# Softmax loop of a fused token-embedding, attention and expert kernel: VectorE's order regrouped, the probabilities' bits moved to ScalarE, two-operand multiplies for the small scalars

## The reference, cut to what matters

```
x_int = x_int - x_int.max(axis=-1, keepdims=True)
x0_int = floor(-0.6931 / scale);  x_int = maximum(x_int, 30 * x0_int)
q = floor(x_int / x0_int);  r = x_int - x0_int * q
exp_int = floor((r * (r + b_int) + c_int) * exp2(30 - q))
sm = round(exp_int.sum(axis=-1, keepdims=True) / exp_int)
big = floor(log2(sm));  big = where(sm - exp2(big) >= exp2(big - 1), big + 1, big)
attn = where(big >= 16, 0, exp2(-clip(big, 0, 15)))
o = attn @ v
```

## Time and profile before

| | us |
|---|---|
| median of three runs | 1189.9 (1189.35 to 1193.78) |
| the profiled execution, its own time | 1189.11 |
| its span | 1187.3 |
| softmax loop, first distances to the end of its barrier | 434.0 to 703.8 |

### The profile page before, as it was taken

The page is one execution under the profiler, slowest core; times in us unless marked ns, Lnnn a source line. Parts: engine busy times, 40 slices in busy tenths (PEclk is TensorE's granted clock), DMA queues, the critical chain, the costliest instruction groups (busy, mean ns, idle before and its releaser), DMA issues.

```text
span 1187.3 us, 25829 instructions
## 1 busy us (share of the span) xinstructions
PE 803.7 (68%) x8714; PEld 613.7 (52%) x8714; DVE 883.3 (74%) x1781; ACT 499.1 (42%) x980; POOL 515.9 (43%) x413
## 2 busy tenths in 40 slices
PE   3898961576077625777778730600739999999998
PEld 2897961455044412444445430200627777777777
DVE  4324424899689969999999976699557777777776
ACT  2222201344454314666666632120415555555554
POOL 1120002587122006666666630633007666666665
PEclk9998995778555555555555555555559999999999
DMA  7544212000022111122112134000000000000000
GB/s 201 154 119 102 63 40 82 22 1 0 12 83 69 54 28 31 28 34 33 28 33 33 21 86 140 0 0 0 10 15 16 23 22 28 28 21 20 28 21 20
DMA packets 112975, 51.84 MB, mean 44 GB/s; under 512 B 75896, under 2 KB 107808, under 8 KB 112928
## 3 DMA queue, kind: packets, MB, share of 16 engines
q1 hardware_dynamic: 111600, 44.94, 15.6%
q0 software_dynamic: 1328, 6.30, 1.9%
HBM read 26.47 MB, written 6.68 MB: 28 GB/s over the span
## 4 chain that ended last, share of the span: by engine, by line
PE 50%; DVE 24%; issue 11%; SPq 5%; DMA 4%; ACT 3%; POOL 2%; DVEq 1%; POOLq 0%; ACTq 0%
PE ps L1267 46%; DVE R L1081 4%; DVE R L1088 2%; DMA R<-h_rows 2%; SPq L435 2%; DVE M L1002 2%; DVE M L1001 2%; DVE R L1094 1%; DVE R L1182 1%; PE ps L1338 1%; SPq L473 1%; ACT R L615 1%; DVE R L991 1%; DVE R L1191 1%; SPq L475 1%
## 5 line engine op out<-in xcount | busy, mean ns | idle before, releaser
L1267 PE MATMUL ps<-R 128*128 128x192 f16 (+9 forms) x3788 | 468.9, 276 | 78.7 <-DVE R L1094 61.3
L1267 PEld LDWEIGHTS ps<-R 128*128 128x128 f16 (+5 forms) x3788 | 356.2, 114 | 170.7 <-issue 77.0
L604 POOL TENSOR_TENSOR R<-R 128x256 f32<-128x256 f32 x238 | 195.5, 828 | 175.0 <-DVE R L1244 173.4
L615 ACT ACTIVATE R<-R,sc 128x884 int16<-128x884 f16 (+13 forms) x135 | 131.3, 1007 | 158.3 <-POOL R L547 41.6
L1267 PE MATMUL ps<-M 32*64 32x68 bf16 (+2 forms) x2048 | 127.0, 252 | 71.0 <-DMA M<-R 53.5
L1244 DVE TENSOR_TENSOR R<-R,ps 64x256 f32<-64x256 f32 (+1 forms) x272 | 113.9, 419 | 63.0 <-ACT R L789 43.7
L1267 PEld LDWEIGHTS ps<-M 32*64 32x64 bf16 (+2 forms) x2048 | 83.8, 136 | 128.8 <-issue 71.7
L789 ACT ACTIVATE R<-ps 128x256 f32<-128x256 f32 x238 | 91.3, 384 | 136.5 <-PE ps L1267 129.5
L612 ACT ACTIVATE R<-ps 68x896 bf16<-68x896 bf16 (+6 forms) x123 | 81.4, 665 | 141.9 <-PE ps L1338 53.2
L612 ACT ACTIVATE R<-R 128x256 f16<-128x256 f32 (+5 forms) x264 | 118.7, 451 | 32.4 <-POOL R L530 20.6
L1251 DVE TENSOR_TENSOR R<-R 128x256 f16<-128x256 f32 x238 | 112.8, 475 | 20.2 <-ACT R L612 18.1
(11 more groups left out here) (217 smaller groups left out, 1098.1 us busy)
## 6 DMA issues: line engine op xcount, KB each, us to landing
R<-in_x_dram SPq DMA_DIRECT2D x12, 576.0 KB, 10.7
M<-R SPq DMA_DIRECT2D x16, 260.0 KB, 2.4
M<-R SPq DMA_DIRECT2D x32, 130.0 KB, 2.1
R<-h_rows SPq DMA_DIRECT2D x4, 816.0 KB
R<-h_rows SPq DMA_DIRECT2D x1, 3264.0 KB, 13.1
R<-R SPq DMA_DIRECT2D x17, 192.0 KB, 2.5
out_dram<-R SPq DMA_DIRECT2D x17, 192.0 KB, 2.0
M<-R SPq DMA_DIRECT2D x128, 12.8 KB
```

Source lines behind the costliest of these rows:

```text
L604: pool.tensor_tensor(hs[0:rows, m % HB, :], hr[0:rows, m % HB, :], other, ALU.mult).then_inc(sem("squared"), 1)
L615: return act.activation(out_, in_, ACT.Identity, scale=scale, bias=bias)
L1267: return pe.matmul(o, a, b, start=start, stop=stop, skip_group_check=True)
```

## The change

VectorE's order in a step becomes: `shares` (lag 3, new), `clamp` (1), `quotients` (1), `totals` (3, was 2), `probabilities` (4), `weights` (2, was 1), `weight_sums` (2), `distances` (0). `prob_bits` leaves VectorE and becomes an activation of ScalarE (Relu with a bias, bf16 to int16) right behind `exponent`; both stand first in ScalarE's step, at lag 4. The third of the sums is made by `shares` as a tensor-by-tensor multiply with a tile of constants, and the two thirds by the same form on GpSimd, at the head of `excess`. `quotient_bits` goes from lag 2 to 3. `excess` no longer waits for `prob_bits`, but for the quotients of the group two ahead, which are those of the same step. `PW` and `sq` are doubled, so `powers` and `squares` wait one group less. Three small memsets are added ahead of the loop.

```diff
-        PW = r0(CW // 2, I16)
-        sq = r0(CW)
+        PW = [r0(CW // 2, I16) for _ in range(2)]
+        sq = [r0(CW) for _ in range(2)]
...
+        thirds = misc(SLOTS)
+        two_thirds = misc(SLOTS)
...
             def excess(g, par, half):
+                pool.wait_ge(sem("wsum"), g + 1)
+                pool.tensor_tensor(S[:, par, 2, :], S[:, par, 0, :], two_thirds, ALU.mult).then_inc(sem("two_thirds"), 1)
                 pool.wait_ge(sem("two_thirds"), g + 1)
-                wait(pool, "pbits", g)
+                wait(pool, "quot", min(g + 3, 32) if isinstance(g, int) else g + 3)
                 wait(pool, "probs", g - 1)
...
-            pipeline(pool, [(excess, 3), (quotient_bits, 2)], 32)
+            pipeline(pool, [(excess, 3), (quotient_bits, 3)], 32)
...
             def powers(g, par, half):
                 act.wait_ge(sem("quot"), g + 1)
-                wait(act, "w", g)
-
-                ident_(PW, Qq[par], scale=-128.0, bias=s1(A_PB)).then_inc(sem("power"), 1)
+                wait(act, "w", g - 1)
+
+                ident_(PW[par], Qq[par], scale=-128.0, bias=s1(A_PB)).then_inc(sem("power"), 1)
 
             def squares(g, par, half):
                 act.wait_ge(sem("rem"), g + 1)
-                wait(act, "w", g)
-                act.activation(sq, rem, ACT.Square, bias=s1(A_BH)).then_inc(sem("sq"), 1)
+                wait(act, "w", g - 1)
+                act.activation(sq[par], rem, ACT.Square, bias=s1(A_BH)).then_inc(sem("sq"), 1)
...
+            def prob_bits(g, par, half):
+                act.wait_ge(sem("exponent"), g + 1)
+                wait(act, "pt_psum", g * 2 - 2)
+
+                act.activation(Pb[par].bitcast(I16), yb[par], ACT.Relu, bias=s1(A_PC)).then_inc(sem("pbits"), 1)
...
-            pipeline(act, [(evac_first, 5), (powers, 1), (squares, 1), (exponent, 3), (evac_o, 7), (evac_second, 5)], 32)
+            pipeline(act, [(exponent, 4), (prob_bits, 4), (powers, 1), (evac_first, 5), (squares, 1), (evac_o, 7), (evac_second, 5)], 32)
...
+            ch(dve.memset(s1(A_PC), -128.0 * 176.0))
+            ch(dve.memset(thirds, 1.0 / 3.0))
+            ch(dve.memset(two_thirds, 2.0 / 3.0))
...
                 wait(dve, "excess", g - 1)
-
-                dve.scalar_tensor_tensor(flat(wv[par]), sq, s1(A_K0), PW.bitcast(BF16), ALU.add, ALU.mult).then_inc(sem("w"), 1)
+                wait(dve, "log2", g - 1)
+
+                dve.scalar_tensor_tensor(flat(wv[par]), sq[par], s1(A_K0), PW[par].bitcast(BF16), ALU.add, ALU.mult).then_inc(sem("w"), 1)
...
+            def shares(g, par, half):
+                dve.wait_ge(sem("wsum"), g + 1)
+                tt(S[:, par, 1, :], S[:, par, 0, :], thirds, ALU.mult).then_inc(sem("third"), 1)
+
             def totals(g, par, half):
-                dve.wait_ge(sem("wsum"), g + 1)
-                ts(S[:, par, 1, :], S[:, par, 0, :], 1.0 / 3.0, None, ALU.mult).then_inc(sem("third"), 1)
-                ts(S[:, par, 2, :], S[:, par, 0, :], 2.0 / 3.0, None, ALU.mult).then_inc(sem("two_thirds"), 1)
                 dve.wait_ge(sem("third"), g + 1)
                 wait(dve, "exponent", g - 1)
...
-            def prob_bits(g, par, half):
-                dve.wait_ge(sem("exponent"), g + 1)
-                wait(dve, "pt_psum", g * 2 - 2)
-
-                ts(Pb[par].bitcast(I16), yb[par], -128.0 * 176.0, 0.0, ALU.add, ALU.max).then_inc(sem("pbits"), 1)
...
-            pipeline(dve, [(clamp, 1), (quotients, 1), (prob_bits, 4), (probabilities, 4), (weight_sums, 2), (totals, 2),
-                           (weights, 1), (distances, 0)], 32)
+            pipeline(dve, [(shares, 3), (clamp, 1), (quotients, 1), (totals, 3), (probabilities, 4),
+                           (weights, 2), (weight_sums, 2), (distances, 0)], 32)
```

More of the change, by code:

```diff
@@ L366, in program @@
          Y_INV, Y_CAPM, T0, T1, T2, G0, G1, A_M16, A_B, A_C, A_K1, A_PB, W_M1, W_M2, W_M3, W_E1, W_E2,
-         W_E3, W_S1, W_S2, W_S3, W_U, G2, G3, G4, W_RU) = range(59)
+         W_E3, W_S1, W_S2, W_S3, W_U, G2, G3, G4, W_RU, A_PC) = range(60)
         QKPARTS = [(yqk[:, 0].rearrange("p (b n) -> p b n", n=N), yqk[:, 1].rearrange("p (b n) -> p b n", n=N),
```

## The result

| | before | changed |
|---|---|---|
| median, us | 1191.84 (4 runs, 1189.35 to 1198.2) | 1248.36 (4 runs, 1245.95 to 1249.89) |
| profiled execution, its own time / span | 1189.11 / 1187.3 | 1247.09 / 1245.3 |
| softmax loop, first distances to the end of its barrier | 434.0 to 703.8 | 437.6 to 761.7 |
| busy: VectorE / ScalarE / GpSimd | 883.3 / 499.1 / 515.9 | 936.3 / 528.6 / 519.6 |

What follows compares the result with a forecast made beforehand. VectorE's and GpSimd's operations exclude each other on a shared resource, full for about 7.8 of the step's 7.83 us. On 1189.1, +53.8 (28 steps) - 2.3 (filling) + 4 (draining) + 0.3 (memsets) gave 1245 us, range 1184 to 1256.

Steps and rivals of the forecast that it cites:

- first rival: VectorE holds the shared resource through its run of operations; steps average 7.9 us, total 1190 (1183 to 1199); chance 0.26.
- forecast mechanism: GpSimd's pending operation enters between two VectorE operations, making the loop's step 9.79 us and the time 1245; chance 0.58.
- 1.: Step's start: totals begin at 0.43 us and let go at 1.35; excess waits from some 0.1 behind the quotients' end.
- 2.: Excess takes the resource from 1.35 to 3.03 us; probabilities wait, end at 3.97 and let go at 3.81.
- 3.: GpSimd's integer subtraction runs from 3.81 to 5.85 us (2.04); the weights wait and end at 6.79.
- 4.: Weight sums depend on the operation just ahead and start at 6.83 us; distances follow 1.00 later at 7.83.
- 5.: Step's end: distances to `shares` 1.36 us (9.19), `shares` 0.12 (9.31), clamp to quotients 0.48, a step of 9.79.
- Filling: Loop's start, up to the fourth quotients: they come at about 455 instead of 457.36 us, -2.3.
- Draining: Loop's end, after the last quotients: +4 us taken, between 0 and +6.8; last probabilities 24.4 after the last quotients.
- second rival: Two SBUF inputs hardly matter: only clamp, quotients and the like exclude GpSimd; -30 us, or about 1158; chance 0.12.
- Relu costs ScalarE something special: ScalarE's bits: Relu costs more than the powers' form, a table exchange in each step; within others, chance 0.04.

Runs made afterwards that it cites:

- e1: The changed kernel, with GpSimd's excess waiting for the weights of the same step instead of its quotients; 1202.8 us, ratio 1.0078 to before.
- e4: The changed kernel, with the waits of probabilities (bits, excess) moved ahead of totals; 1246.4 us in one execution.
- e5: The changed kernel, with the bits back on VectorE right ahead of probabilities; 1256.0 us in one execution.
- e3: The kernel before, with third and two thirds of the sums as tensor-by-tensor multiplies on VectorE; 1199.8 us in one execution.
- e2: The kernel before, with the bits on ScalarE and excess waiting for the same step's quotients; 1180.6 us, in a second set 1179.5 (ratio 0.9904).
- e6: The kernel of e2, with the two thirds made by GpSimd at the head of excess; 1179.85 us, ratio 0.9897 to before.
- e11: The kernel of e9, with SyncE's spreading of v one step later in its own order; 1178.7 us, ratio 0.9895 to before.
- e9: The changed kernel, VectorE reordered with distances behind totals, thirds on ScalarE, subtraction also waiting for weights, scores one step ahead; 1256.9 us, ratio 1.0563 to before.

## Why the prediction was right

Forecast: 1245, slower with 0.68, in a range of 1184 to 1256 that takes in the first rival; the forecast mechanism's own range was 1234 to 1256. Measured: 1248.4, inside both. By its own steps, with the timeline of the changed kernel, 0 at 603.57:

1. Quotients to totals 0.43: 0.43. Excess starts to wait 0.1 behind the quotients: 604.24, 0.16 behind.
2. Excess ends at 3.03: 3.02. Probabilities end at 3.97: 3.96. Its duration alone, estimated as 1.68: 1.67 in e1.
3. Subtraction ends at 5.85: 5.87. Weights end at 6.79: 6.80.
4. Weight sums at 6.83: 6.84. Distances at 7.83: 7.83.
5. `shares` at 9.19: 9.07. This is the term that was off. The 1.36 from distances to the clamp in the earlier trace rows contains the clamp's wait for the last distances, behind whose end it starts (653.31 against 653.28); `shares` has no such wait, starts before their end (612.64 against 612.72) and follows in 1.24. So the step is 9.68, not 9.79, and 28 steps +50.6, not +53.8.

Filling -2.6 (-2.3). Draining +6.3, where I took +4 and 6.8 was the upper end: the last probabilities end 24.6 after the last quotients (24.4 by the working), after 4.06 us of waiting for ScalarE's bits, and what follows them takes 7.65 to the barrier's end, hardly less than the 8.36 of before. The sum of the loop, +55.5 forecast with the +4, was +54.3. The 3.4 us that the profile has more ahead of the loop, in stages with the same code, were not foreseen. So a step too long by 0.11 (3.2 us), draining too short by 2.3 and these 3.4 nearly cancel: that the total came within 3.5 us is in part luck, while the steps of the list came out one by one.

The choice that decided, that GpSimd's pending operation enters between two operations of VectorE, rested on one tiny reduction; that it would hold for operations of 1.7 and 2 us was a bet, at 0.58. All of e1, e4 and e5 bear it out. The first rival, that VectorE holds on, fell with the 2.54 and 2.92 us. Its working had a right part: without GpSimd at the seams the bits' chain shows by 0.3 to 0.5 us, and e1 showed 0.38. The second rival, that two inputs hardly matter, fell with the same rows and with e3. That Relu costs ScalarE something special did not come true: its bits take 1.03 us, like the powers.

On the sides named in the prediction: by the rule of the Trainium skill ("SBUF — State Buffer", Who interferes with whom) the one that issues first has the resource, and e4's and e5's rows agree (in e4 excess starts at 612.88, probabilities at 613.62; in e5 excess at 609.13, bits at 609.88). That section of the Trainium skill also says that the first keeps it for the whole instruction; here the excess of e4 began work 0.93 us after the start of totals, which are shown as 1.07 long. By the rule for relu of the Trainium skill ("ScalarE: Activation LUTs", Rules for kernel authors) the bits should have stayed on VectorE; the operation is 0.65 us longer on ScalarE, and yet moving it gained 0.42 us a step in e2, because what it leaves is the resource that both engines fight for.

What stays open: why the quotients follow the clamp by 0.04 us in one step and 0.13 in the next (it does so in before, e2 and e6); and whether three buffers of weights, which would let weights stand one lag earlier, bring the step under 7.4. No run bears on either.

## What to carry to other kernels

Before regrouping the operations of two engines that exclude each other, mark each operation as on or off the shared resource, and ask at each seam between two that are on it whether the other engine has one pending: it will go in, and the order should put an operation that is off the resource behind that seam. An engine that is busy for 98% may be waiting inside its instructions, which shows when the same instruction is compared with one that ran alone. Taking an operation off the resource can be worth more than keeping it where it is fastest.

## What the runs showed that I had not expected

- An operation that waits for the holder's semaphore starts 0.15 us after the holder's end and, by the 0.92 us after which it lets go, 0.36 after the release (e11), while one that is already pending starts work at the release (the changed kernel: subtraction ends 1.91 after the probabilities that let it in, of its 2.05).
- A transfer can become the bound by its place in a queue alone: moving the spreading of v by one step in SyncE's order gained 78 us (e9 to e11).
- The stages ahead of the loop, with the same code, differ by 12 us between profiles (first quotients at 435.8 in before, at 447.7 in the second set of e2), twice the 6 us taken as what a measurement can tell. From a single execution only the stage in question can be compared.
